# A 0/1 table of destinations, built per group of 512 edges from bytes, and two loads moved in SP's queue

## The reference

```python
h = jnp.maximum(_layernorm(x, axis=-1), 0.0)
concat = jnp.concatenate([h[src], h[dst], edge_attr], axis=-1)   # 96 + 96 + 64
gates = jax.nn.sigmoid(concat @ W_e + b_e)
messages = jax.nn.softplus(concat @ W_n + b_n)
gated = gates * messages
h_new = jax.ops.segment_sum(gated, dst, num_segments=n)
edge_count = jnp.clip(jax.ops.segment_sum(ones, dst, n), 1.0, None)[:, None]
return x + (h + h_new / edge_count)
```

## Time and profile before

| | us |
|---|---|
| median of 3 runs (947.77 to 948.77) | 948.62 |
| the profiled execution | 951.04 |
| its span, from the first to the last instruction | 949.3 |

### The profile page before, as it was taken

One profiled execution on the slowest core, in us unless ns is written; L12 is line 12 of the kernel. 1 busy time (PEld: TensorE's weight loads), 2 busy tenths in 40 slices (PEclk: granted clock), 3 DMA queues, 4 the chain that ended last, 5 costly groups with the idle time before them and its releaser, 6 DMA issues.

```text
span 949.3 us, 15042 instructions
## 1 busy us (share of the span) xinstructions
PE 605.9 (64%) x3832; PEld 578.3 (61%) x3832; DVE 546.1 (58%) x2203; ACT 520.5 (55%) x1330; POOL 512.4 (54%) x404
## 2 busy tenths in 40 slices
PE   0255777667656765775776677567667657758971
PEld 0255777567556765764766566567667656747871
DVE  5667466466546645654664665466466456548551
ACT  0356655655564565466456546645655654665660
POOL 5211355654565466466556546655654664666676
PEclk9997778878777787778787778778778777878795
DMA  8277757766785677687577668767866865875652
GB/s 202 55 176 162 156 126 166 161 138 141 159 158 125 151 165 149 132 176 154 124 165 164 137 136 173 152 122 160 164 143 148 165 150 125 182 150 121 113 82 18
DMA packets 285403, 136.32 MB, mean 144 GB/s; under 512 B 262207, under 2 KB 275848, under 8 KB 285320
## 3 DMA queue, kind: packets, MB, share of 16 engines
q1 hardware_dynamic: 249214, 116.34, 52.8%
q0 software_dynamic: 34576, 18.40, 14.4%
q10 hardware_dynamic: 1530, 0.61, 0.3%
HBM read 88.16 MB, written 48.30 MB: 144 GB/s over the span
## 4 chain that ended last, share of the span: by engine, by line
DMA 33%; SPq 26%; DVE 26%; issue 8%; PE 3%; POOL 2%; DVEq 0%; ACT 0%; POOLq 0%; ACTq 0%
DMA dst_across<-dst_pad 30%; SPq L324 11%; SPq L297 10%; DVE stats L703 9%; DVE node_out L801 9%; SPq L314 6%; DVE messages L725 3%; DVE onehot L762 3%; POOL out L417 2%; DMA low_across<-low_pad 2%; PE pick_ps L950 1%; DVE same_prev L735 1%; DVE dst_t L645 1%; DMA dst_t<-dst_pad,first_tile_i 1%; DMA dst_t<-in_src 1%
## 5 line engine op out<-in xcount | busy, mean ns | idle before, releaser
L417 POOL DMA_INDIRECT out<-final,scatter_idx x196 | 309.7, 1580 | 317.9 <-DVE final L717 251.1
L962 PE MATMUL sums_ps<-messages,same 128*128 128x97 f32 x392 | 123.3, 415 | 247.5 <-DVE messages L725 247.5
L484 ACT ACTIVATE node_out<-node_x,shift,rstd 128x96 f32<-128x96 f32 x637 | 261.7, 458 | 12.5 <-DVE shift L756 12.5
L396 POOL DMA_INDIRECT edge_x<-in_x,src_idx x196 | 200.6, 1023 | 111.2 <-issue 58.8
L962 PEld LDWEIGHTS sums_ps<-messages,same 128*128 128x128 f32 x392 | 99.7, 312 | 254.1 <-DVE messages L725 254.0
L732 DVE TENSOR_TENSOR same<-dst_across,dst_col 128x512 f32<-128x512 int32 x49 | 34.0, 693 | 327.6 <-DMA dst_across<-dst_pad 327.6
L950 PE MATMUL pick_ps<-onehot,node_out 128*96 x1568 | 165.2, 263 | 61.0 <-ACT node_out L484 44.9
L950 PEld LDWEIGHTS pick_ps<-onehot,node_out 128*96 128x96 f32 x1568 | 156.6, 178 | 77.5 <-issue 77.2
L490 ACT ACTIVATE log_var<-var 128x20 f32<-128x20 f32 x52 | 11.4, 218 | 321.1 <-DVE var L827 321.1
L703 DVE BATCH_NORM_STATS2 stats<-node_x 128x6 f32<-128x96 f32 x784 | 142.2, 243 | 0.0
L963 PE MATMUL sums_ps<-messages,same_prev 128*128 128x97 f32 x392 | 118.4, 402 | 0.0
(11 more groups left out here) (107 smaller groups left out, 624.1 us busy)
## 6 DMA issues: line engine op xcount, KB each, us to landing
node_x<-in_x SPq DMA_DIRECT2D x48, 768.0 KB, 5.2
out<-node_out SPq DMA_DIRECT2D x48, 768.0 KB, 7.8
low_across<-low_pad SPq DMA_DIRECT2D x98, 200.0 KB, 6.0
dst_across<-dst_pad SPq DMA_DIRECT2D x49, 256.0 KB, 6.2
attr<-in_edge_attr SPq DMA_DIRECT2D x48, 128.0 KB, 6.4
edge_x<-in_x,src_idx POOLq DMA_INDIRECT x196, 2.8
out<-final,scatter_idx POOLq DMA_INDIRECT x196, 6.1
node_x<-in_x SPq DMA_DIRECT2D x1, 624.0 KB
```

The lines of the kernel that those rows point to most:

```text
L396: nc.gpsimd.indirect_dma_start(out=edge_x[i % NS][:, t, :], out_offset=None, in_=x, in_offset=bass.IndirectOffsetOnAxis(ap=src_idx[:, i * ...
L417: nc.gpsimd.indirect_dma_start(out=out, in_=final[j % FINALS][:, t, :], in_offset=None, out_offset=bass.IndirectOffsetOnAxis(ap=scatter_id ...
L484: last = nc.scalar.activation(node_out[n % NS][:, r, :], node_x[n % NS][:, r, :], ACT.Relu, bias=shift[us][:, c:c + 1], scale=rstd[us][:, ...
L962: nc.tensor.matmul(sum_ps[:, t, :], same[:, t, :], cur, start=True, stop=False)
```

## The change

The table is no longer made per half chunk from that half's first edge, but per group of 512 edges (GROUP), fixed stretches of the edge list. There are 50 groups (one of padding), and four of them stand in a ring, `onehot` [128, 2048 + 64]; the 64 columns behind the end repeat the start. The low bits are stored and loaded as bytes, one DMA of 64 KB a group from a fixed place, into three buffers. DVE makes groups 0 and 1 in its step -2, then group i+3 in step i. PE now needs two places per block: `to` in pick_ps as before, and `of` in the ring; it loads 16 registers for each half. `places` works out a position `near` for each half, the first edge held within bounds about the even line of 256 edges per half, and a difference between it and the true one counts as a violation. In SP's queue, low_across of group i and dst_across of step i-6 (it was i-7) are issued ahead of node_x and the store; its loop has one step less. On POOL the look_i gather is ahead of the first gathers; on ACT the store of the low bits is ahead of the weights' loads. The small tiles of `places` move into a part of dst_t that is still free then.

```diff
+GROUP = TB * P
+GROUPS = STEPS + 1
+SLOTS = 4
+RING = SLOTS * GROUP
+BEHIND = GROUP
+BEYOND = (AHEAD * GROUP) - GROUP // 2 - SPAN
+CELLS = 2 * BLOCKS + 1
+LOWS = 3
...
-        low_across = sb("low_across", [P, 2, SPAN])
-        onehot = [sb(f"onehot{v}", [P, 2, SPAN]) for v in range(2)]
+        low_across = [sb(f"low_across{v}", [P, GROUP], U8) for v in range(LOWS)]
+        onehot = sb("onehot", [P, RING + WINDOW])
...
         @block.sync
-            def load_low(n):
-                first, second = (first_at(sp, first_row[0:1, 2 * n + h:2 * n + h + 1]) for h in range(2))
-                wait(sp, onehot_done, n)
-                for h, at in ((0, first), (1, second)):
-                    sp.dma_start(low_across[:, h, :],
-                                 low_flat[bass.ds(at, SPAN)].partition_broadcast(P)).then_inc(low_loaded, 16)
+            def load_low(g):
+                wait(sp, onehot_done, g - LOWS + 1)
+                sp.dma_start(low_across[g % LOWS][:, :],
+                             low_flat[g * GROUP:(g + 1) * GROUP].partition_broadcast(P)).then_inc(low_loaded[g % LOWS], 16)
...
                 if runs_step(j):
                     wait(sp, node_sum_done, j + 1)
+                if NS <= i < GROUPS:
+                    load_low(i)
+                k = i - 6
+                if runs_step(k):
+                    if k == 0:
+                        sp.wait_ge(dst_stored, 16)
+                    wait(sp, same_done, 2 * (k - 1))
+                    sp.dma_start(dst_across[k % 2][:, :, :].rearrange("p t e -> p (t e)"),
+                                 dst_flat[k * GROUP:(k + 1) * GROUP].partition_broadcast(P)).then_inc(across_loaded[k % 2], 16)
                 if runs_step(i):
                     move_chunk(sp, i, x, node_x[i % NS], True, node_loaded[i % NS])
                 if runs_step(j):
                     move_chunk(sp, j, out, node_out[j % NS], False, node_stored[j % NS])
...
-                if i == NS - 1:
-                    sp.wait_ge(place_done, 2)
-                    sp.dma_start(first_row[0:1, :].rearrange("a (p b) -> a p b", b=1),
-                                 place_i[0:HALVES, BLOCKS:BLOCKS + 1]).then_inc(place_loaded, 16)
-                    sp.dma_start(place_row[0:1, :].rearrange("a (p b) -> a p b", b=BLOCKS),
-                                 place_i[0:HALVES, 0:BLOCKS]).then_inc(place_loaded, 16)
-                    sp.wait_ge(place_loaded, 32)
+                if i == 2:
                     sp.wait_ge(low_stored, 16)
-                    load_low(0)
-                n = i - 2
-                if i >= NS - 1 and runs_step(n):
-                    load_low(n)
-
-                k = i - 7
-                if runs_step(k):
-                    if k == 0:
-                        sp.wait_ge(dst_stored, 16)
-                    wait(sp, same_done, 2 * (k - 1))
-                    sp.dma_start(dst_across[k % 2][:, :, :].rearrange("p t e -> p (t e)"),
-                                 dst_flat[k * TB * P:(k + 1) * TB * P].partition_broadcast(P)).then_inc(across_loaded[k % 2], 16)
-
-            for i in range(STEPS + 7):
+                    for g in range(LOWS):
+                        load_low(g)
+                if i == 3:
+                    sp.wait_ge(place_done, 3)
+                    sp.dma_start(place_row[0:1, :].rearrange("a (p b) -> a p b", b=CELLS),
+                                 place_i[0:HALVES, :]).then_inc(place_loaded, 16)
+                    load_low(i)
+
+            for i in range(STEPS + 6):
...
         @block.vector, in places()
+                nc.vector.tensor_scalar(place_f[:, :], below[:, 0:BLOCKS], below[:, 0:1], float(REACH), ALU.subtract, ALU.min)
+                link(nc.vector.scalar_tensor_tensor(out=first_f[:, :], in0=first_tile[:, :], scalar=float(P),
+                                                    in1=below[:, 0:1], op0=ALU.mult, op1=ALU.add))
+                nc.vector.tensor_copy(place_i[:, 0:BLOCKS], place_f[:, :]).then_inc(place_done, 1)
+                per_half = GROUP / 2.0 / (BLOCKS * P)
+                nc.vector.tensor_scalar(least[:, :], bound[:, 0:1], per_half, HALVES * GROUP / 2.0, ALU.mult, ALU.min)
+                link(nc.vector.tensor_scalar(most[:, :], bound[:, 0:1], per_half, float(BEYOND), ALU.mult, ALU.add))
+                link(nc.vector.tensor_tensor(most[:, :], first_f[:, :], most[:, :], ALU.min))
+                link(nc.vector.scalar_tensor_tensor(out=near_f[:, :], in0=least[:, :], scalar=-float(BEHIND), in1=most[:, :],
+                                                    op0=ALU.add, op1=ALU.max))
+                nc.vector.tensor_copy(place_i[:, 2 * BLOCKS:CELLS], near_f[:, :]).then_inc(place_done, 1)
+                link(nc.vector.tensor_scalar(place_i[:, BLOCKS:2 * BLOCKS], place_f[:, :], near_f[:, 0:1], None, ALU.add))
+                nc.vector.tensor_scalar(place_i[:, BLOCKS:2 * BLOCKS], place_i[:, BLOCKS:2 * BLOCKS], RING - 1, None,
+                                        ALU.bitwise_and).then_inc(place_done, 1)
+                nc.vector.tensor_scalar(crowd[:, BLOCKS + 1:BLOCKS + 2], first_f[:, :], near_f[:, 0:1], 2.0 * WINDOW,
+                                        ALU.not_equal, ALU.mult)
...
-            def one_hot(n):
-                wait(dve, low_loaded, 32 * (n + 1))
-                wait(dve, pick_done, 2 * (n - 1))
-                nc.vector.tensor_scalar(onehot[n % 2][:, :, :], low_across[:, :, :], lane[:, 0:1], None,
-                                        ALU.is_equal).then_inc(onehot_done, 1)
+            def one_hot(g):
+                u = g % SLOTS
+                wait(dve, low_loaded[g % LOWS], 16 * (g // LOWS + 1))
+                wait(dve, pick_done, 2 * (g - SLOTS + 2))
+                last = nc.vector.tensor_scalar(onehot[:, u * GROUP:(u + 1) * GROUP], low_across[g % LOWS][:, :], lane[:, 0:1], None,
+                                               ALU.is_equal)
+                if u == 0:
+                    last = nc.vector.tensor_scalar(onehot[:, RING:RING + WINDOW], low_across[g % LOWS][:, 0:WINDOW], lane[:, 0:1],
+                                                   None, ALU.is_equal)
+                last.then_inc(onehot_done, 1)
...
-                if runs_step(n):
-                    one_hot(n)
+                for g in (0, 1) if i == -2 else (i + 3,):
+                    if 0 < i + 3 and g < GROUPS:
+                        one_hot(g)
...
         @block.tensor
+            def places_of(half):
+                pe.load(place_regs, place_row[0:1, half * CELLS:half * CELLS + 2 * BLOCKS])
+                to = [pe.snap(r, min_val=0, max_val=REACH) for r in place_regs[:BLOCKS]]
+                of = [pe.snap(r, min_val=0, max_val=RING - 1) for r in place_regs[BLOCKS:]]
+                return to, of
...
-                    last = nc.tensor.matmul(pick_ps[0:D, bass.ds(a, WINDOW)], node_out[d % NS][:, h * BLOCKS + b, :],
-                                            onehot[d % 2][:, h, bass.ds(a, WINDOW)], start=True, stop=True)
+                    last = nc.tensor.matmul(pick_ps[0:D, bass.ds(to[b], WINDOW)], node_out[d % NS][:, h * BLOCKS + b, :],
+                                            onehot[:, bass.ds(of[b], WINDOW)], start=True, stop=True)
...
-                    wait(pe, onehot_done, d + 1)
+                    wait(pe, onehot_done, d + 2)
...
-                    picks(d, 1, at)
+                    picks(d, 1, places_of(2 * d + 1))
```

More of the change, by code:

```diff
@@ L6 @@
 I32 = mybir.dt.int32
+U8 = mybir.dt.uint8
 ALU = mybir.AluOpType
@@ L76, in build @@
         flag = sb("flag", [P, 1], I32)
[L78 to L83, removed]
         dst_col = sb("dst_col", [P, 1 + TILES])
@@ L103, in build @@
         low_i = room(2 * P, I32).rearrange("p (b e) -> p b e", b=2)
-        low_f = room(2 * P).rearrange("p (b e) -> p b e", b=2)
+        low_u = room(2 * P // 4, U8).rearrange("p (b e) -> p b e", b=2)
         broken, real, ahead = (room(2 * P).rearrange("p (b e) -> p b e", b=2) for _ in range(3))
         coarse = room(TILES)
+        tiles_below, first_tile, first_f, near_f, least, most = (room(1) for _ in range(6))
+        first_tile_i = room(1, I32)
+        below, crowd, place_f = room(BLOCKS + 1), room(BLOCKS + 2), room(BLOCKS)
+        place_i = room(CELLS, I32)
         look_i = room(LOOK, I32)
@@ L195, in build @@
         across_loaded = sems("across_loaded", 2)
[L196 removed]
+        low_loaded = sems("low_loaded", LOWS)
         gathered = sems("gathered")
@@ L311, in build, with first_at @@
         low_flat = low_pad.rearrange("t e -> (t e)")
-        def first_at(eng, cell):
-            return eng.value_load(cell, min_val=0, max_val=TILES * P)
+        def first_at(eng, half):
+            cell = half * CELLS + 2 * BLOCKS
+            return eng.value_load(place_row[0:1, cell:cell + 1], min_val=0, max_val=TILES * P)
         @block.sync
@@ L389, in step @@
             def step(i):
+                if i == 0:
```

(36 more changed lines are left out.)

11 lines of the change are left out of this document (4 added, 7 removed).

## The result

The median went from 948.26 us (947.77 to 948.77, 4 runs) to 985.08 us (981.17 to 986.82, 4 runs), a ratio of 1.0382 with a 95% interval of 1.0349 to 1.0416. The forecast was 732. The profiled execution has a span of 982.4 us and a mean granted clock of 0.737.

A forecast was written before the change was run, and what follows sets the result against it. The kernel was taken as bound by waits, through DVE, for dst_across, and POOL as the next bound: first scatter at 87.5, 43 rounds of 13.8 (593.4), 45 for six scatter groups and the end gave 732 us, range 682 to 800.

The forecast's parts named there:

- PE: Second half's 16-register load between attr transposes and second picks: bounded by 0 and 1 us a step, taken as 0.
- Rival 3: PE clock stays low, at 1.2 GHz PE needs 18.9 us a step, 967 us in all; chance 0.03.
- dst_across a step sooner: Load issued ahead of node_x and out serves step s+2; DVE's 7.64 us wait before `same` goes to nothing.
- low_across, SP: SP's queue: one 64 KB load replaces two of 200 KB; under 6 us of issues a step.
- The table: DVE's onehot instruction of 512 columns instead of 800: 0.5 us, between 0.40 and 0.69.
- POOL's collisions: POOL's gathers or scatters blocked by DVE's node_out: 13.8 us a step instead of 12.4 undisturbed.
- DVE waiting for gathers: Sign of being right: DVE now waits for POOL's gathers ahead of L806.
- The granted clock: Sign of being right: PE's granted clock above 0.9, full clock expected nearly throughout.
- POOL's busy share: Sign of being right: POOL's busy share goes from 54% to 75% or more.
- The beginning: Start of the kernel up to `final` of step 0: 86 us instead of 107.84, early steps 9 to 12 us.
- the 732.6 of the sum: Forecast span: first scatter at 87.5, 43 rounds 593.4, last six scatter groups 45, then 6.7 to the end.
- rival 2: DMA is the bound: 2.44 MB a step take 14.8 to 16.3 us, 777 to 842 us; chance 0.20.

The follow-up runs named there:

- e1_cells20: The changed kernel with 20 instead of 17 words a half in place_row, so each load of 16 registers starts at a multiple of 16 bytes; 741.53 us.
- e11_cells20_off16: The changed kernel with 20 words a half and the whole place_row moved by four words (16 bytes); 745.30 us.
- e2_before_off4: The kernel before with place_row moved by one word, so each load of 16 registers starts 4 bytes past a multiple of 16; 954.83 us.
- e4_cells18: The changed kernel with 18 words a half, so each step's first load is aligned and the second is 8 bytes off; 916.12 us.
- e5_two_banks: The changed kernel with 20 words a half and both register loads at the step's start, into two banks of 16 registers; 734.78 us.

## Why the prediction was wrong

**The step that failed is *PE.*** It bounded the load of 16 registers by 0 and 1 us a step and took 0, for want of a row on PE. There was such a row, the load of the kernel before (1.1 us), which I did not look for, since busy views leave sequencer instructions out. Even with it the forecast would have failed: the load was aligned there, and CELLS = 17 in the diff made three of four unaligned, 3.8 to 6.3 us. Two such loads a step, the second with nothing to hide it, together with the half clock after each stop, made the step 18.6 us ((936.30 - 118.58) / 44, from the first `final` to the 45th) instead of 13.8. Against the 13.4 of e1_cells20 these are 5.2 us more, in two nearly equal parts: PE stood idle ahead of the picks for 241.5 us in all instead of 107.7 (2.7 a step), and was busy for 682.0 us instead of 562.7 with the same 3832 matmuls at a lower clock (2.4 a step).

**Rival 3 was the nearest,** slower than before by PE at half clock, but for another reason: I let PE be idle only for lack of work, while it was kept from its work and lost its clock by that. The mean granted clock fell to 0.737, and the slices of the page show mostly 6 and 7.

**What the aligned kernel shows of the other steps.** With twelve bytes more a half the time is 741.53 us (e1_cells20) and 745.30 (e11_cells20_off16), against 732 forecast and 682 to 800 as the range:

- *dst_across a step sooner:* right; 7.64 us of wait a step went to nothing, also in the changed kernel.
- *low_across, SP:* right in that no wait for either is left. But SP's issues came to 8.1 us a step in e1_cells20, not under 6: the store's issue takes 3.7 us now and attr's 3.2 (medians; before, 1.6 and 0.4). Both stand behind what is urgent, as said.
- *The table:* the 512 columns from bytes took 0.47 us, forecast 0.5, bounds 0.40 and 0.69.
- *POOL's collisions:* right in kind, and the step nearly right in size. Node_out now runs beside POOL; in e1_cells20 (timeline):

```profile
406.92 1.57 POOL L420 DMA_INDIRECT out<-final,scatter_idx  x1 [0.30 <-issue]
...
408.53 1.76 DVE L822 TENSOR_TENSOR node_out<-node_out,node_x 128x1536 f32<-128x1536 f32 x1 [0.94 <-PE pick_ps L977]
...
408.80 2.92 POOL L420 DMA_INDIRECT out<-final,scatter_idx  x1 [0.30 <-issue]
...
412.02 1.55 POOL L420 DMA_INDIRECT out<-final,scatter_idx  x1 [0.30 <-issue]
```

A scatter that began 0.27 us into node_out took 2.92 us instead of 1.57. The trace shows the rule: 40 transfers began inside a node_out, and of those that began over 0.1 us into it each scatter ended 1.43 to 1.52 us after node_out's end and each gather 0.82 to 0.90, however early they had begun. The 35 that were already under way when node_out began took at most 1.79 us. From the first scatter (100.31) to the end of the last (731.74), less 45 for the last six groups, 43 rounds took 13.6 us each; forecast 13.8, from the two late steps of the earlier trace rows. The means of scatters and gathers rose from 1580 and 1023 ns to

```profile
L420 POOL DMA_INDIRECT out<-final,scatter_idx x196 | 328.3, 1675 | 84.0 <-issue 58.7
L406 POOL DMA_INDIRECT edge_x<-in_x,src_idx x196 | 211.1, 1077 | 95.9 <-issue 57.6
```

- *DVE waiting for gathers:* wrong. DVE waits for picks, and PE's chain runs at 13.4 us a step ((685.22 - 40.32) / 48 of node_out), just under POOL, where 9.7 at full clock were counted. The granted clock was 0.86, not above 0.9, with PE still stopping ahead of the second picks. POOL's busy share was 73%, not 75 or more.
- *The beginning:* first `final` at 98.78, not 86:

```profile
11.30 1.16 POOL L397 DMA_INDIRECT dst_t<-dst_pad,dst_t  x1 [9.29 <-DMA dst_pad<-dst_t]
...
98.78 0.55 DVE L732 TENSOR_TENSOR final<-sums_ps,inv_count 128x384 f32<-128x384 f32 x1
...
100.31 1.63 POOL L420 DMA_INDIRECT out<-final,scatter_idx  x1 [21.36 <-DVE final L732]
```

The gather of look_i started at 11.30, not at 9.9, because it waits for the store of dst_pad; and the first steps were at 12.3 to 14.6 us instead of 9 to 12, PE's picks at half clock among them. This adds 12.8 us, and the 43 rounds at 13.6 instead of 13.8 take 7 off; together they are the 5.9 by which the span of e1_cells20, 738.5, lies above the 732.6 of the sum. So the near hit of the aligned kernel is in part two errors of opposite sign.
- *DMA as the bound* (rival 2): not seen; 173 GB/s over 200 to 700 us at a share of 0.80.

## What to carry to other kernels

Where a table of small records is read into many registers at once, pad the record so that each load starts at a multiple of 16 bytes (985 against 742 us here), and look for sequencer instructions by their line, as the busy views leave them out. A load of registers in the middle of an engine's queue is a wait like any other: ask what hides it. Loads 4.7 us longer cost 10 us in all where the engine had a wait further on (e2_before_off4); second loads 2.6 us longer on the median cost 175 where it had none (e4_cells18 against e1_cells20). When a ring has several parts in series, one part alone may be worth far less than its share (taking away 327.6 us of wait for dst_across gave 115), and a change that opens them all makes visible what was hidden under the slack.

## What of the hardware was not expected

- A load of 16 registers on PE took 1.1 us from a 16-byte boundary at a step's start and 3.8 to 6.3 us from 4, 8 or 12 bytes past one. Boundaries of 64 bytes were not needed: e1_cells20 has 80 bytes a half.
- The aligned loads in the middle of a step took 2.5 us on the median and up to 3.2, at its start 1.1 to 1.3 but for two; with both at the start (e5_two_banks) both had a median of 1.1. Why the place matters stays open.
- ACT's loads of a single register from the same row, three in four of them off a 16-byte boundary too, had a median of 0.28 us (0.27 to 1.15), and nearly the same at each distance from a boundary (0.28 to 0.29). So of the loads seen here only that of 16 words suffers.
- Cutting node_out in four made the sum only 0.2 us longer (1.97 instead of 1.76) and took most of POOL's long scatters away (from 17 over 1.9 us to 3), but the time of the kernel did not fall.
